# Sorting the edges of a graph layer on TensorE: two of five value parts moved to ScalarE, keys stored as two 16-bit numbers, 52 instead of 50 columns, 10 instead of 18 idle matmuls

## The reference, cut to what matters

```python
src = rel_pair_idx[:, 0]; dst = rel_pair_idx[:, 1]
m = jnp.maximum(jnp.max(weighting_gate), jnp.float32(0.0))
exp_e = jnp.exp(weighting_gate - m)
row_sum = jax.ops.segment_sum(exp_e, src, num_segments=n_nodes)
atten_e = exp_e / (row_sum[src] + 1e-06)
Mfeat = source_features @ Wm + bm
out0 = jax.ops.segment_sum(atten_e[:, None] * Mfeat[dst], src, num_segments=n_nodes)
out1 = jax.ops.segment_sum(atten_e[:, None] * Mfeat[src], dst, num_segments=n_nodes)
```

## Time and profile before

| | |
|---|---|
| median of 3 runs | 523.14 us (523.12 to 523.48) |
| the profiled execution's own time | 522.98 us |
| its span in the profile | 520.7 us |
| PE, DVE, ACT, POOL busy | 464.6, 414.9, 256.7, 198.8 us |

### The profile page before, as it was taken

The page is one execution under the profiler, slowest core; times in us unless marked ns, Lnnn a source line. Parts: engine busy times, 40 slices in busy tenths (PEclk is TensorE's granted clock), DMA queues, the critical chain, the costliest instruction groups (busy, mean ns, idle before and its releaser), DMA issues.

```text
span 520.7 us, 8981 instructions
## 1 busy us (share of the span) xinstructions
PE 464.6 (89%) x2877; PEld 372.4 (72%) x2877; DVE 414.9 (80%) x793; ACT 256.7 (49%) x682; POOL 198.8 (38%) x159
## 2 busy tenths in 40 slices
PE   4189999999988999989999999989999847999992
PEld 1167878888867887967666666588988745788881
DVE  6969999999988887979999999578639857265562
ACT  0596566666661110003666666675345482466650
POOL 0088878688876888840000000000000006345322
PEclk9789999999999999999999999989999957899998
DMA  7980000000000000013000000000003992343210
GB/s 188 292 284 3 1 3 2 3 3 2 3 1 2 3 1 3 2 34 148 1 2 1 2 2 2 1 1 0 1 1 103 432 311 66 100 119 102 85 60 15
DMA packets 15840, 31.08 MB, mean 60 GB/s; under 512 B 7750, under 2 KB 8381, under 8 KB 14773
## 3 DMA queue, kind: packets, MB, share of 16 engines
q1 hardware_dynamic: 9237, 23.21, 13.3%
q0 software_dynamic: 6560, 7.32, 7.2%
HBM read 24.90 MB, written 7.38 MB: 62 GB/s over the span
## 4 chain that ended last, share of the span: by engine, by line
PE 40%; POOL 32%; issue 11%; DVE 8%; DMA 4%; SPq 3%; ACT 2%; DVEq 0%; POOLq 0%; ACTq 0%
POOL slots L454 31%; PE banks L693 16%; PE banks L840 6%; PE banks L532 5%; PE banks L712 3%; SPq L375 2%; PE banks L685 2%; PE banks L705 2%; PE banks L831 1%; PE banks L494 1%; DMA x_rows<-factors 1%; DVE rec L1274 1%; DVE stat L1276 1%; DMA rec<-x_rows,get_i 1%; PE banks L850 1%
## 5 line engine op out<-in xcount | busy, mean ns | idle before, releaser
L454 POOL DMA_INDIRECT slots<-record,row_i x120 | 161.6, 1346 | 68.4 <-issue 68.4
L465 POOL DMA_INDIRECT rec<-x_rows,get_i x17 | 20.0, 1176 | 207.0 <-DMA x_rows<-factors 202.1
L693 PE MATMUL banks<-d_hot,s_hot 128*128 128x251 bf16 x648 | 92.1, 276 | 0.9 <-DVE s_hot L1207 0.9
L1525 ACT ACTIVATE adj<-banks x108 | 63.7, 590 | 37.0 <-PE banks L693 36.8
L693 PEld LDWEIGHTS banks<-d_hot,s_hot 128*128 128x128 bf16 x648 | 54.4, 98 | 9.5 <-issue 1.0
L532 PE MATMUL banks<-w_hi,xT_hi 128*125 128x512 f32 (+1 forms) x160 | 59.5, 372 | 0.8 <-DVE bia L1045 0.4
L532 PE MATMUL banks<-w_hi,xT_lo 128*125 128x512 f32 (+1 forms) x160 | 58.6, 366 | 0.0
L532 PE MATMUL banks<-w_lo,xT_hi 128*125 128x512 f32 (+1 forms) x160 | 58.5, 366 | 0.0
L1207 DVE TENSOR_TENSOR s_hot<-s_one,parts 128x1024 bf16<-128x1024 bf16 (+1 forms) x84 | 51.0, 656 | 0.0
L1470 ACT ACTIVATE q_sb<-q_sb,hmax 125x64 f32<-125x64 f32 x80 | 26.7, 336 | 39.8 <-DVE hmax L1064 39.8
L532 PEld LDWEIGHTS banks<-w_hi,xT_hi 128*125 128x125 f32 x160 | 29.7, 185 | 7.1 <-issue 1.6
(11 more groups left out here) (299 smaller groups left out, 1065.9 us busy)
## 6 DMA issues: line engine op xcount, KB each, us to landing
w_raw<-in_w2f SPq DMA_DIRECT2D x4, 1024.0 KB, 9.1
w_raw<-in_wqkv SPq DMA_DIRECT2D x3, 1024.0 KB, 18.9
rec<-in_x SPq DMA_DIRECT2D x2, 1120.0 KB
x_rows<-rec SPq DMA_DIRECT2D x10, 224.0 KB
w1a<-in_w1f SPq DMA_DIRECT2D x1, 2048.0 KB, 8.5
w1b<-in_w1f SPq DMA_DIRECT2D x1, 2048.0 KB, 16.6
b_sb<-in_b2f SPq DMA_DIRECT2D x1, 2048.0 KB, 22.2
slots<-record,row_i POOLq DMA_INDIRECT x120, 2.6
```

Source lines behind the costliest of these rows:

```text
L454: pool.indirect_dma_start(slots, bass.IndirectOffsetOnAxis(ap=row_i[:, c:c + 1], axis=0), record[:, c, :], None).then_inc(slot_st, 16)
L465: pool.indirect_dma_start(rec_c[:, c % RING, :], None, x1_rows, bass.IndirectOffsetOnAxis(ap=get_i[:, c:c + 1], axis=0)).then_inc(ld_rec[c ...
L693: mm = pe.matmul(flat_banks[:, bass.ds(at_in, AW)], s_hot[:, n % DB, i, q, :, j], d_hot[:, n % DB, q, :, j], start=False, stop=(i == WT - ...
L1525: act.activation(adj[:, bass.ds(w, BW2)], flat_banks[0:TP, bass.ds(out_at, BW2)], ACT.Copy).then_inc(win_ok, 1)
```

## The change

It does five things.

1. `row_1h` for value parts 0 to 2 (`VD` = 3) is made by VectorE as before, in one instruction of 125 x 3 x 128 x 2. Parts 3 and 4 are made by ScalarE: for each of the two columns and each of the two parts one copy of `row_one` (125 x 128) with the value as a per-partition scale (`act_parts`). TensorE waits for both. VectorE may write a buffer of `row_one` again only when ScalarE has read it too.
2. The key is no longer one number, but two bfloat16 numbers in the same four bytes: `src % 125` and `dst % 250` (`record_b`, `got_b`). The sorted sum has three groups (two keys and the weight, the latter in another bank), and `parts` 0 and 1 come from one addition each.
3. 52 columns are sorted on TensorE, so 26 pairs instead of 25, and 118 indirect DMAs instead of 120.
4. `RUN_UP` is 10 instead of 18.
5. Some semaphores are merged or dropped, and `rest` is made behind the first `s_one` instead of ahead of it.

```diff
-PCOLS = 50
+PCOLS = 52
 P0 = EC - PCOLS
-RS, VT = 6, 5
+RS, VT, VD = 6, 5, 3
-RUN_UP = 18
+RUN_UP = 10
...
             sp.wait_ge(sort_hot, PCOLS // 2)
+            sp.wait_ge(sort_act, PCOLS // 2)
             sp.dma_start(w1_sb[0][:, :, :], w1f[:, 0:KD // 2, :]).then_inc(ld_w1, 16)
...
             for n in range(PCOLS // 2):
                 pe.wait_ge(sort_hot, n + 1)
+                pe.wait_ge(sort_act, n + 1)
                 for j in range(2):
                     for v in range(VT):
-                        k = 0 if v < 2 else 1
-                        mm = pe.matmul(bank[1][:, k * NCH:(k + 1) * NCH], row_1h[:, n % RS, v, :, j], chunk_1h[:, n % RS, :, j],
...
+                        to = bank[1][:, v * NCH:(v + 1) * NCH] if v < 2 else bank[0][:, 0:NCH]
+                        mm = pe.matmul(to, row_1h[:, n % RS, v, :, j], chunk_1h[:, n % RS, :, j],
...
             for _ in range(RUN_UP):
-                pe.matmul(bank[0][:, 0:WIN], ident, const("cols"), start=True, stop=True)
+                pe.matmul(bank[IDLE_IN][:, 0:WIN], ident, const("cols"), start=True, stop=True)
...
-            dve.scalar_tensor_tensor(s_lo[:, :], s_hi[:, :], -float(TP), src_i[:, :], ALU.mult, ALU.add)
-            own_step(dve.scalar_tensor_tensor(record[:, :, 0], d_hi[:, :], -float(WIN), dst_i[:, :], ALU.mult, ALU.add))
-            dve.scalar_tensor_tensor(record[:, :, 0], s_lo[:, :], float(KEY), record[:, :, 0], ALU.mult,
-                                     ALU.add).then_inc(key_ok, 1)
+            dve.scalar_tensor_tensor(record_b[:, :, 0], s_hi[:, :], -float(TP), src_i[:, :], ALU.mult, ALU.add).then_inc(key_ok, 1)
+            dve.scalar_tensor_tensor(record_b[:, :, 1], d_hi[:, :], -float(WIN), dst_i[:, :], ALU.mult, ALU.add).then_inc(key_ok, 1)
...
                 if n >= 2:
                     dve.wait_ge(sort_hot, n - 1)
-                own_step(dve.tensor_tensor(row_one[:, n % 2, :, :], col_2[0:TP, 0:CH, :], of_pair(at_2[:, 0, :], n, CH), ALU.is_equal))
+                    dve.wait_ge(sort_act, n - 1)
+                dve.tensor_tensor(row_one[:, n % 2, :, :], col_2[0:TP, 0:CH, :], of_pair(at_2[:, 0, :], n, CH),
+                                  ALU.is_equal).then_inc(sort_one, 1)
...
             def sort_parts(n):
-                shape = [TP, VT, CH, 2]
...
+                shape = [TP, VD, CH, 2]
+                dve.wait_ge(sort_one, n + 1)
+                dve.tensor_tensor(row_1h[:, n % RS, 0:VD, :, :], row_one[:, n % 2, :, :].unsqueeze(1).to_broadcast(shape),
+                                  sort_v[:, 0:VD, 2 * n:2 * n + 2].unsqueeze(2).to_broadcast(shape), ALU.mult).then_inc(sort_hot, 1)
...
             dve.wait_ge(ld_got, 16)
-            own_step(dve.tensor_tensor(table[:, :, :], got[:, :, :].rearrange("p c k -> p k c"),
-                                       bank[1][:, 0:RW * NCH].rearrange("p (k c) -> p k c", k=RW), ALU.add))
...
+            for k in range(2):
+                dve.tensor_tensor(parts[:, k, :], got_b[:, :, k], bank[1][:, k * NCH:(k + 1) * NCH], ALU.add)
+            dve.tensor_tensor(table[:, :], got[:, :, 1], bank[0][:, 0:NCH], ALU.add).then_inc(table_ok, 1)
+            dve.wait_ge(table_ok, 1)
...
+            def act_parts(n):
+                act.wait_ge(sort_one, n + 1)
+                if n >= RS:
+                    act.wait_ge(sort_ps, n - RS + 1)
+                for j in range(2):
+                    for v in range(VD, VT):
+                        last = act.activation(row_1h[:, n % RS, v, :, j], row_one[:, n % 2, :, j], ACT.Copy,
+                                              scale=sort_f[:, v - VD, 2 * n + j:2 * n + j + 1])
+                last.then_inc(sort_act, 1)
             for t in range(NT):
...
+                if t >= 2 and t % 2 == 0:
+                    act_parts(t // 2 - 1)
+            for n in range(NT // 2 - 1, PCOLS // 2):
+                act_parts(n)
```

More of the change, by code:

```diff
@@ L42 @@
 RW = 2
-KEY = 256
-PCOLS = 50
+PCOLS = 52
 EARLY = 6
 P0 = EC - PCOLS
-RS, VT = 6, 5
+RS, VT, VD = 6, 5, 3
 DIV = 1049
@@ L181, in build @@
         at_2 = place("at_2", E0 + 5496, [TP, 2, PCOLS], BF16)
-        sort_v = place("sort_v", E0 + 5560, [TP, VT, PCOLS], BF16)
-        sort_r = place("sort_r", E0 + 5720, [TP, PCOLS])
+        sort_v = place("sort_v", E0 + 5560, [TP, VD + 1, PCOLS], BF16)
+        sort_r = place("sort_r", E0 + 5664, [TP, PCOLS])
+        sort_f = place("sort_f", E0 + 5720, [TP, VT - VD, PCOLS])
         upto = place("upto", E0 + 6672, [128, NB])
@@ L199, in build @@
         got = place("got", 32216, [128, NCH, RW])
-        table = place("table", 32648, [128, RW, NCH])
-        key_i = place("key_i", 33080, [128, 2, NCH], I32)
+        got_b = got[:, :, :].bitcast(BF16)
+        table = place("table", 32648, [128, NCH])
         rest = place("rest", 33512, [128, NCH])
@@ L448, in _ @@
             pool.wait_ge(w_exp, 1)
-            pool.wait_ge(key_ok, 1)
+            pool.wait_ge(key_ok, 2)
             for i, (a, b) in enumerate(LOTS):
@@ L497, in _ @@
             mm.then_inc(count_ps, 1)
-            pe.wait_ge(top_val, 1)
-            pe.matmul(bank[4][0:TP, 0:1], ones[0:1, 0:TP], top[0:1, 2:3], start=True, stop=True).then_inc(top_bc, 1)
+            pe.wait_ge(top_col, 2)
+            pe.matmul(bank[4][0:TP, 0:1], ones[0:1, 0:TP], top[0:1, 2:3], start=True, stop=True).then_inc(top_row, 1)
             pe.wait_ge(count_ok, 1)
@@ L652, in _ @@
                 pe.wait_ge(sort_hot, n + 1)
+                pe.wait_ge(sort_act, n + 1)
                 for j in range(2):
                     for v in range(VT):
-                        k = 0 if v < 2 else 1
-                        mm = pe.matmul(bank[1][:, k * NCH:(k + 1) * NCH], row_1h[:, n % RS, v, :, j], chunk_1h[:, n % RS, :, j],
-                                       start=(n == 0 and j == 0 and v == 0), stop=(n == PCOLS // 2 - 1 and j == 1 and v in (1, VT - 1)),
-                                       skip_group_check=True)
+                        to = bank[1][:, v * NCH:(v + 1) * NCH] if v < 2 else bank[0][:, 0:NCH]
+                        mm = pe.matmul(to, row_1h[:, n % RS, v, :, j], chunk_1h[:, n % RS, :, j],
+                                       start=(n == 0 and j == 0 and v in (0, 2)),
+                                       stop=(n == PCOLS // 2 - 1 and j == 1 and v in (0, 1, VT - 1)), skip_group_check=True)
                 mm.then_inc(sort_ps, 1)
@@ L806, in _ @@
             both(route, 4)
-            pe.wait_ge(oh_ok, 1)
+            pe.wait_ge(route_ok, 1)
             for t in range(NT):
@@ L982, in _ @@
             for t in range(DT):
-                norm_stats(t)
+                last = norm_stats(t)
+            own_step(last)
             def chunk_tables():
@@ L1140, in sort_parts @@
             def sort_parts(n):
-                shape = [TP, VT, CH, 2]
-                dve.tensor_tensor(row_1h[:, n % RS, :, :, :], row_one[:, n % 2, :, :].unsqueeze(1).to_broadcast(shape),
-                                  sort_v[:, :, 2 * n:2 * n + 2].unsqueeze(2).to_broadcast(shape), ALU.mult).then_inc(sort_hot, 1)
+                shape = [TP, VD, CH, 2]
+                dve.wait_ge(sort_one, n + 1)
+                dve.tensor_tensor(row_1h[:, n % RS, 0:VD, :, :], row_one[:, n % 2, :, :].unsqueeze(1).to_broadcast(shape),
+                                  sort_v[:, 0:VD, 2 * n:2 * n + 2].unsqueeze(2).to_broadcast(shape), ALU.mult).then_inc(sort_hot, 1)
             for t in range(NT):
@@ L1197, in _ @@
                                   values(0).to_broadcast([128, k, CH, 2]), ALU.is_equal).then_inc(one_ok, 1)
+                if n == 0:
+                    dve.wait_ge(part_ok, 1)
+                    dve.tensor_tensor(rest[:, :], table[:, :], parts[:, 2, :], ALU.subtract).then_inc(rest_ok, 1)
                 if n >= DB:
@@ L1241, in _ @@
                     dve.tensor_tensor(out_lo[:, :, 0:GH], msg[:, :, 0:GH], out_hi[:, :, :], ALU.subtract).then_inc(out_split, 1)
-                dve.tensor_tensor(rec[:, t, :], rec[:, t, :], bias("p"), ALU.add).then_inc(bp_ok, 1)
+                last = dve.tensor_tensor(rec[:, t, :], rec[:, t, :], bias("p"), ALU.add)
+            own_step(last)
             def hid_var(w):
```

79 lines of the change are left out of this document (35 added, 44 removed).

## The result

| | before | after |
|---|---|---|
| median | 523.31 us (523.12 to 523.57, 4 runs) | 517.2 us (515.22 to 517.82, 4 runs) |
| the profiled execution's own time, span | 522.98, 520.7 us | 517.81, 515.9 us |
| PE, DVE, ACT, POOL busy | 464.6, 414.9, 256.7, 198.8 us | 462.1, 407.5, 287.9, 193.8 us |

The ratio is 0.988, interval [0.985, 0.991]. The sign was as forecast; the time is 2.1 us under the forecast of 519.3 and 0.8 us under the range.

The account below looks back on a forecast made before the run. The GpSimd queue's indirect DMAs were taken as the bound, with the VectorE-paced sort equally long. First batch 4.20 us earlier, 0.4 lost to the clock: -3.8 from 522.98, so 519.2, or 519.3 as median; range 518.0 to 521.5.

Parts of the forecast that it names:

- The sign: Whole kernel: faster by more than 1.05 us, chance 0.90; within that 0.03, slower 0.07.
- the slower rival: Sort on ScalarE: copies don't overlap, 1.58 us a pair, kernel at 525.7 us; chance 0.08.
- Two DMAs fewer: GpSimd queue at the sort's end: 118 indirect DMAs instead of 120 bring the landing of `got` 3.33 us sooner.
- The join: VectorE between `got` and first batch: three additions and a later `rest` gain 0.87 us.
- The run-up: Idle matmuls on TensorE ahead of the first batch: eighteen would make the batch 1.9 us late, ten end in time.
- the queue's pace: GpSimd queue during the sort: DMA starts were 1.69 us apart; the sum counted no gain from a faster pace.
- The rival: Faster GpSimd queue: DMAs at 1.48 us, 0.4 us gained, up to 1.3 if ScalarE's pair is 1.17; chance 0.10.
- the sort's end at 230.8: Sort's last matmul: ends at 230.8 us, 0.4 us ahead of `got`, and would be last if the queue sped up.
- ScalarE's pair: Four copies per pair in the sort: 1.22 us taken, bounds 1.1 and 1.58; the skill page's estimate was 1.17.
- the moved wait: VectorE in the sort: waiting for `row_one` one instruction later gains some 0.1 us a pair.
- The clock term of 0.4: TensorE at the first batch: 0.4 us lost to a lower clock after 1.4 us idle, bounds 0 and 1.3.
- The price of the rival: Clock falls at the first batch: full cost 1.3 us, kernel at 520.2 us; chance 0.20.

Follow-up runs that it names:

- c4: The changed kernel run again without any edit, as the measure for other runs on its chip: 515.37 us, ratio 0.986.
- a2: The changed kernel run again without any edit: 515.6 us, ratio 0.985.
- b2: The changed kernel with all five value parts on VectorE and the wait for `row_one` back ahead of `chunk_1h`: 520.88 us, ratio 0.999.
- a3: The changed kernel with all five value parts made by VectorE: 533.7 us, ratio 1.022.
- b1: The kernel before with only the wait for `row_one` moved, from ahead of `chunk_1h` to ahead of `row_1h`: 539.79 us, ratio 1.037.
- b4: The changed kernel with VectorE making part 3 too in every third pair from pair 6 on: 529.39 us, ratio 1.015.
- c3: The changed kernel with VectorE's wait for `row_one` put back ahead of `chunk_1h` as well: 518.5 us, ratio 0.990.
- b3: The changed kernel with 50 columns instead of 52, so 120 indirect DMAs: 521.96 us, ratio 0.998.
- c2: The changed kernel with 50 columns, so 120 indirect DMAs, and 17 idle matmuls instead of 10: 522.99 us, ratio 0.999.
- a1: The kernel before run again without any edit: 522.65 us, ratio 0.9998.

## Why the prediction was right in sign and short in size

*What held.* ScalarE's copies overlap, and the slower rival (no overlap) is excluded. Two DMAs fewer: 3.33 us in after and c4, 3.21 in a2. The join: 0.90 us gained for 0.87, and 5.42 us to the batch for 5.45. The run-up: necessary, 1.9 us as said.

*The step that failed: the queue's pace.* The sum kept the queue at its old pace during the sort. It stood among the rivals with 0.10, and it is what came: stretch b is 1.1 to 1.6 us shorter (26.31, 25.99, 25.83 against 27.44), and with all parts on VectorE it is 27.42 again (b2). The rival was also too small. It let the sort's end at 230.8 absorb nearly all of the gain, but from its start to its end the sort took 26.04 us in a2 and c4, where the forecast had 26.8 (204.0 to 230.8). The term that was mis-sized there is ScalarE's pair: 1.18 us measured (23.55 / 20), 1.22 taken. Twenty pairs make 0.8 us of it, and the forecast's own formula then gives 1.22 + 23.55 + 0.15 + 1.14 = 26.06. The lower of the prediction's two estimates, 1.17, was the nearer one. TensorE's 25.7 us for 26 pairs are close below. In after the sort took 27.33 and did hold the join, by some 1.7 us: 229.88 against 228.2 for `got`; in a2 `got` was last by 0.2 us, in c4 the two end together (229.1 and 229.2). So both paths move, and which of them is last differs between executions.

The cause under it I had only half seen. The prediction wrote that VectorE has no gap at this time, but the earlier trace rows has one of 0.04 us (226.88 to 226.92). What a3, b1 and b4 share is VectorE without a gap between instructions with two SBUF inputs, and one indirect DMA stood for 12 to 19 us until the first gap. What before, after, b2 and c3 share is a short gap in nearly every pair: from its own wait, or from waiting for ScalarE or TensorE. Of the DMAs of the sort, the 110th needs such a gap; why it, and not the three before it, is not shown. And where the gaps are longer, the queue's pace is faster (c3 against c4). The Trainium skill, "SBUF — State Buffer", SBUF: two separate sides, has an exclusive lock on a port pair that VectorE holds also with two SBUF inputs, against a GpSimd operation that reads SBUF; the runs agree with its direction. The page speaks of a wait for one whole instruction. The 107th to 109th DMAs of a3, 0.2 to 0.5 us longer than the undisturbed 1.19, would fit that; the 110th, held for up to 19 us while each VectorE instruction starts before the last ends, does not; the measurement decides. That it is this lock is the page's explanation, and no row shows the port. I took the moved wait for 0.1 us gained a pair; alone it is the 17.8 us loss of b1, and only because ScalarE's share makes VectorE wait did it do no harm. That was luck, not insight.

*The clock term of 0.4* was not paid: from the run-up's end to the batch 1.27 us pass in after, 1.28 in c4 and 1.45 in a2, the clock stayed at 1.00, and f is 99.05, 99.05 and 99.04. The price of the rival, 1.3 us, is what c3 lost after 1.97 us (f 100.36, clock 0.63), so the forecast's upper bound was right.

*Terms that the sum left out.* The time around the span is shorter, 1.85 to 1.97 us in after's repeats and 2.2 to 2.5 in nearly all runs of before. The kernels with 120 indirect DMAs (b3 and c2 too: 2.2 to 2.3) have the long one, those with 118 mostly the short one: 0.35 us by the profiled executions. In b2, with 118, six of ten executions have 2.2 to 2.4, so the count alone does not decide it, and the cause is open. And in some executions of before, as a1, the long run-up holds the batch, 1.2 us that the shorter one saves; I had asked only what eighteen would cost the new kernel.

*The sum by what was measured,* c4 against before: b -1.45, c -3.33, d +0.37, e -0.90, f -0.16, h -0.35, together -5.8 us; a2 gives -5.65 and after -4.57, where the forecast was -3.8. From -3.8 to -5.8, the queue less what the sort's end takes back is 1.1 us (b and d), the clock that was not paid 0.4, the time around the span 0.35, the rest f and roundings. The medians differ by 6.1, 7.05 and 7.5 us in the three series. Against a1, the other profile of before, the same stretches give -6.9 to -8.2, for its held batch (e) and a longer c. The medians lie between the two, so no further cause is needed, though with so few profiles none is excluded: the landing of x (a) and the end of the program (g, 178.9 to 181.5 in after's executions) vary by as much.
